# A gated cross-attention and expert layer on one core: the end of the attention reordered, the routing lists built in f16 pairs

## The chip, the core and the metric

The kernel runs on one core of one Trainium2 chip. The metric is the device time of one execution in microseconds (us). A core has TensorE (PE in the rows; PEld is its weight load), VectorE (DVE), ScalarE (ACT), GpSimd (POOL) and SyncE (SP), each with its own list of instructions, kept in step by semaphores; the DMA engines move data beside them.

## What is computed

Inputs: x (4 x 512 x 256, so 2048 tokens), a context of 4 x 1601 rows, for every token an index into its context, two gates, and weights. In short:

```python
# x = x + tanh(g_xattn) * attention(layernorm(x))
q = heads(layernorm(x) @ Wq.T)                       # 16 heads of 16
k, v = split(ctx @ Wkv.T)
rows = clip(index - [0, 1, 2, 3], 0)                 # 4 keys and values for a token
x = x + tanh(g0) * (softmax(q . k[rows] / 4) @ v[rows]) @ Wo.T
# x = x + tanh(g_ffn) * experts(layernorm(x))
p = softmax(layernorm(x) @ gate_w.T)                 # 8 experts, the best 2 of each token
for e in range(8):
    out += p_e * (silu(xn @ w1[e] + b1[e]) @ w2[e] + b2[e])
```

The indices of this input lie below 128, so only the first 128 context rows of each batch are projected.

## The kernel before, in words

**Tiles.** Tokens lie in T = 16 tiles of 128, on the partitions. Matrix products of the attention and of the router run in f32; those of the experts run in f16 with both factors split into a high and a low half.

**Start.** Keys and values of the first 128 context rows are projected for each batch b (PE line 813), copied from PSUM (ACT lines 632 and 692 for b = 0 and 2, VectorE line 1114 for 1 and 3) and stored to `near_rows_b` in DRAM (SP line 406). For every tile, GpSimd then issues a gather (line 515) of 128 windows of four rows, 1 MB, into one of 8 slots. Gathers 0 to 3 go out one behind the other, then the norms of tiles 4 to 15 (lines 467 to 473) are made, then gather u + 4 in step u. Gather 4 waits for all four stores (line 511). SP holds the first expert weights back until the four stores have landed (line 418).

**Attention loop, step t.** VectorE multiplies keys by queries (1128), reduces them to scores (1132), masks, takes the maximum and subtracts it; ScalarE takes Exp (651); VectorE normalizes (1153 to 1158); GpSimd multiplies the values by the probabilities (490; the second half of the last tile is VectorE's, 1165). TensorE turns and sums them in 16 matmuls (859, `aT`), ScalarE copies aT (670), TensorE projects (872), VectorE adds it to the residual `xs` (1146) and takes the statistics of the second norm (1149, 1169). GpSimd finishes that norm (495 to 503), ScalarE applies it (662: `x2`) and casts the high half (666), GpSimd makes the low half (525), ScalarE issues the store of the token to `tokens_split` (642). TensorE turns x2 (846), ScalarE copies it (686), TensorE makes the logits (838), ScalarE keeps them (681). Every engine runs this from one `step(t)`, with the lags of `second(t)`, `router(t)` and `norms_at(t)` (lines 296 to 323), up to t = T + 2; LATE = 12 is the tile from which the lags are shorter. Each step of SP, GpSimd, ScalarE and TensorE is thus an order fixed by the lags, and an engine stands at the first wait of that order that isn't met.

**Routing.** VectorE runs a chain of instructions that each wait for the one before (`link`): for the tiles below LATE, then for the last four, maximum, difference, Exp (ScalarE, 656 and 708), sum, the best two experts, one-hots (`choose`, 1188). TensorE counts members (901, 902), VectorE scans (1221) and derives how many tiles of 128 each expert fills, their order by size (1226 to 1237), and every token's slot, column (tile) and row (1240 to 1251). The list "which token is in which slot" is a matrix product of one-hots of 32 (tile, choice) pairs: rows (`row_tok`, 27 by VectorE in 1269, 5 by ScalarE in 723) times columns (1264) multiplied by the token number (GpSimd, 563). GpSimd also makes three small tables (555 to 558) and padding rows. TensorE sums the lists (910), VectorE makes `slot_row` (1285 to 1290). At the end a further chain finds for each tile the expert above its own (1293 to 1314 on VectorE, 937 and 939 on TensorE, `e_from` 747 on ScalarE, `e_prev` 566 on GpSimd).

**Experts.** Up to NT = 39 tiles; 37 are filled here. GpSimd gathers the tokens of a tile (587), TensorE turns them (991), VectorE copies them (1334, `xT`), TensorE multiplies up (963) and down (977 to 985), ScalarE applies silu (759), VectorE splits the result (1323, 1325) and weights it (1348, 1351), GpSimd adds it to the output in DRAM (595). The weights arrive in f32 (SP, 371: 16 transfers) and are split in 32 units: ScalarE the high half (739), VectorE the low half (1308), two units ahead of the first tile and then one a tile. The split starts only when all weights are there (`w_in`, 742).

```python
# line 510, GpSimd, gather of tile u
if u == 4:
    for b in range(1, B):
        pool.wait_ge(s[f"kv_out{b}"], 16)
# line 1269, VectorE, one-hots of the rows
count(v.tensor_tensor(row_tok[:, first:last, :], spread_mid(iota[:, :], n),
                      r_row[:, first:last].rearrange("p (n o) -> p n o", o=1).to_broadcast([P, n, P]),
                      ALU.is_equal))
```

## Time and profile before

| | us |
|---|---|
| median of 3 runs | 382.8 (382.32 to 383.78) |
| the profiled execution, its own time | 385.14 |
| its span, first to last instruction | 383.4 |
| TensorE busy | 313.2 (82%) |
| VectorE busy | 273.8 (71%) |
| GpSimd busy | 214.9 (56%) |
| ScalarE busy | 174.4 (45%) |

Busy shares are means over stages that differ much. The mean granted TensorE clock is 0.907 of full speed; 1.00 is 2.4 GHz, 0.5 is 1.2 GHz. In a row of the timeline the first number is the start in us from the span's start, the second the duration, then engine, line, operation, output<-input, and in brackets how long the engine was idle before it and what released it. A merged row (x16) gives the time from its first start to its last end.

### The profile page before, as it was taken

To read this page: it belongs to the slowest core of one execution; us is meant where nothing else is said; L and a number is where in the kernel's file an instruction comes from. 1 tells how busy PE (TensorE), PEld (TensorE's weight loads), DVE (VectorE), ACT (ScalarE), POOL (GpSimd) and SP (SyncE) were. 2 spreads that over 40 slices of the span, in tenths; PEclk is the share of its full clock that TensorE was granted. 3 is DMA by queue.
4 is the path that set the end of the run, shared out by engine and by line. 5 is a ranking of instruction groups with operands and counts; after the bars stand their busy time and mean duration, and the time that the engine had idled before them with its cause. 6 is when DMAs were issued, how large, how long until landed. Compare 5 with 4: busy or idle time off the path is not lost.

```text
span 383.4 us, 10814 instructions
## 1 busy us (share of the span) xinstructions
PE 313.2 (82%) x3163; PEld 255.6 (67%) x3163; DVE 273.8 (71%) x636; ACT 174.4 (45%) x490; POOL 214.9 (56%) x234
## 2 busy tenths in 40 slices
PE   3753999999885121999999999999999999999830
PEld 3432888888773120988888888888888888777610
DVE  3856699999914884597878778887787887565510
ACT  2430255555434253565556556555654644344200
POOL 1365588886763184526574766667477566633240
PEclk9985999999976555799999999999999999999985
DMA  7598999999599800203332342323233233222121
GB/s 224 194 358 331 383 358 335 412 350 363 169 345 376 263 1 22 54 14 59 43 57 45 45 66 38 58 39 59 49 53 46 47 57 56 40 52 29 19 29 14
DMA packets 31388, 53.20 MB, mean 139 GB/s; under 512 B 4818, under 2 KB 25538, under 8 KB 29284
## 3 DMA queue, kind: packets, MB, share of 16 engines
q0 software_dynamic: 9408, 26.63, 27.7%
q1 hardware_dynamic: 16100, 22.57, 17.0%
q10 hardware_dynamic: 5824, 3.26, 2.8%
q8 instruction: 33, 0.54, 0.6%
q14 instruction: 23, 0.19, 0.1%
HBM read 42.29 MB, written 10.17 MB: 137 GB/s over the span
## 4 chain that ended last, share of the span: by engine, by line
PE 70%; POOL 7%; issue 7%; DVE 5%; DMA 4%; ACT 3%; POOLq 0%; SPq 0%; ACTq 0%; DVEq 0%
PE ps L963 25%; PE ps L977 14%; PE ps L980 7%; PE ps L859 6%; PE ps L872 3%; DMA near_rows<-w_parts 2%; PE ps L991 2%; PE ps L813 2%; POOL sel L490 2%; PE ps L985 2%; PE ps L831 2%; DMA w_parts<-in_L_xattn_Wkv 1%; PE ps L838 1%; ACT aT L670 1%; PE ps L984 1%
## 5 line engine op out<-in xcount | busy, mean ns | idle before, releaser
L963 PE MATMUL ps<-sel,w_parts 128*128 128x128 f16 x1776 | 142.1, 221 | 0.6 <-DVE sel L1334 0.6
L963 PEld LDWEIGHTS ps<-sel,w_parts 128*128 x1776 | 120.7, 99 | 25.1 <-issue 0.9
L759 ACT ACTIVATE sel<-ps,b1T 128x128 f32<-128x128 f32 x296 | 84.5, 369 | 92.2 <-PE ps L963 86.2
L595 POOL DMA_INDIRECT out<-sel x37 | 62.9, 1700 | 87.7 <-DVE sel L1351 72.2
L977 PE MATMUL ps<-w_parts,sel 128*128 x259 | 96.3, 379 | 2.0 <-DVE sel L1325 1.7
L980 PE MATMUL ps<-w_parts,sel 128*128 x259 | 70.6, 273 | 0.0
L1325 DVE SCALAR_TENSOR_TENSOR sel<-sel 128x512 f16<-128x512 f32 x74 | 51.3, 693 | 2.5
L587 POOL DMA_INDIRECT sel<-tokens_split,sel x37 | 44.8, 1210 | 7.5 <-POOL sel L582 5.9
L1308 DVE SCALAR_TENSOR_TENSOR w_parts<-w_parts x32 | 39.0, 1220 | 9.2 <-issue 7.9
L582 POOL TENSOR_TENSOR sel<-sel 128x1 f32<-128x1 f32 x37 | 39.3, 1062 | 2.4 <-PE ps L991 2.4
L1323 DVE TENSOR_SCALAR sel<-sel 128x512 f16<-128x512 f32 x74 | 33.6, 455 | 9.3 <-ACT sel L759 9.2
L739 ACT ACTIVATE w_parts<-w_parts x32 | 33.9, 1067 | 10.2 <-issue 5.3
L1334 DVE COPY sel<-ps 128x512 f16<-128x512 f16 x37 | 15.7, 425 | 30.8 <-PE ps L991 21.2
L977 PEld LDWEIGHTS ps<-w_parts,sel 128*128 128x128 f16 x259 | 25.3, 98 | 7.5 <-issue 2.9
L980 PEld LDWEIGHTS ps<-w_parts,sel 128*128 128x128 f16 x259 | 25.3, 98 | 3.5
L872 PE MATMUL ps<-WT,aT 128*128 128x256 f32 x64 | 18.9, 420 | 4.7 <-ACT aT L670 4.5
L859 PE MATMUL ps<-ident,sel 128*128 128x128 f32 x128 | 17.5, 294 | 5.9 <-POOL sel L490 5.9
L859 PEld LDWEIGHTS ps<-ident,sel 128*128 128x128 f32 x128 | 16.6, 208 | 6.8 <-POOL sel L490 6.6
L831 PE MATMUL ps<-WT,xnT 128*128 128x256 f32 x64 | 17.6, 399 | 4.0 <-ACT xnT L676 4.0
L1348 DVE TENSOR_SCALAR xn<-ps,sel 128x256 f32<-128x256 f32 x37 | 17.7, 479 | 3.0 <-PE ps L985 2.9
L1146 DVE SCALAR_TENSOR_TENSOR xs<-ps,tanh_g,xs 128x256 f32<-128x256 f32 x16 | 7.6, 476 | 16.2 <-PE ps L872 16.2
L525 POOL TENSOR_TENSOR xsplit<-x,xsplit 128x256 f16<-128x256 f32 x16 | 11.2, 703 | 14.1 <-ACT xsplit L666 13.0
(215 smaller groups left out, 470.2 us busy)
## 6 DMA issues: line engine op xcount, KB each, us to landing
w_parts<-in_L_ffn_w SPq DMA_DIRECT2D x16, 1024.0 KB
out<-xs SPq DMA_DIRECT2D x16, 128.0 KB
tokens_split<-xsplit ACTq DMA_DIRECT2D x16, 128.0 KB, 5.9
xs<-in_x SPq DMA_DIRECT2D x3, 512.0 KB, 11.2
near_rows<-w_parts SPq DMA_DIRECT2D x4, 256.0 KB, 6.9
sel<-tokens_split,sel POOLq DMA_INDIRECT x37
out<-sel POOLq DMA_INDIRECT x37
w_parts<-in_ctx ACTq DMA_DIRECT2D x1, 512.0 KB, 4.0
```

The source lines that it names most:

```text
L582: pool.tensor_tensor(slot_w[:, at(q + 1)], xg[(k + 1) % 4][:, bass.ds(e + D, 1)], valid[:, at(q + 1)], ALU.mult).then_inc(s["slot_w_ok"], 1)
L587: pool.indirect_dma_start(xg[k], None, xd, bass.IndirectOffsetOnAxis(slot_row[:, at(q + 4)], 0))\
L595: pool.indirect_dma_start(out_rows, bass.IndirectOffsetOnAxis(slot_row[:, at(q - 1)], 0), y_sb[(k + 3) % 4], None, compute_op=ALU.add).the ...
L739: act.activation(part(to, 0), place(raw), ACT.Copy, scale=W_SCALE).then_inc(s["w_hi_ok"], 1)
L759: act.activation(h32[n][:, c * P:c * P + P], ps_h[n][:, c * P:c * P + P], ACT.Silu, bias=biases[:, c:c + 1], scale=1.0 / (X_SCALE * W_SCALE))\
L859: mm = pe.matmul(ps_a[:, c * P:c * P + P], slot(t - 1)[:, j, D + c * P:D + c * P + P], ident[:, :], start=(j == 0), stop=(j == WIN - 1))
L963: mm = pe.matmul(ps_h[n][:, c * P:c * P + P], w, xx, start=(i == 0), stop=(i == len(products) - 1))
L977: pe.matmul(sides, hi, both, start=(c == 0), stop=False)
L980: mm = pe.matmul(ps_y[n][:, 0:D], lo, rhi, start=False, stop=False)
L1308: v.scalar_tensor_tensor(out=part(to, 1), in0=place(raw), scalar=W_SCALE, in1=part(to, 0), op0=ALU.mult, op1=ALU.subtract).then_inc(s["w_l ...
L1323: v.tensor_scalar(h_hi[n][:, cols], h32[n][:, cols], H_SCALE, None, ALU.mult).then_inc(s["hhi_ok"], 1)
L1325: v.scalar_tensor_tensor(out=h_lo[n][:, cols], in0=h32[n][:, cols], scalar=H_SCALE, in1=h_hi[n][:, cols], op0=ALU.mult, op1=ALU.subtract). ...
```

## The change

- **Start.** ScalarE copies batches 0 and 1, VectorE 2 and 3. Gather 4 waits for its own store only (batch 1). Gather 0 goes out, then the norms of tiles 4 to 15, then gathers 1 to 3. SP no longer holds the first weights back; weights 11 to 15 go out in step 13, when the last gather has landed, 7 to 10 as their slots come free. Two small VectorE instructions (`gate2`, `b2_lo`) move behind step 0.
- **Drain.** `step(t)` runs to tile 14; what follows is written out as a list of calls on each engine. Turns and logits of the last four tiles use PSUM banks of their own.
- **Routing.** The scan runs on VectorE over the one-hots before the members are counted; sums and the rank matrix are accumulated in PSUM by TensorE (`ps_members`, `ps_row`, `ps_base`), two links of VectorE's chain go. The one-hots of rows and columns and the product with the token number are made by VectorE with f16 operands, laid out so that two neighbours lie next to each other (`spread_pairs`, `over_pairs`). The tables move to VectorE, the padding to ScalarE and TensorE; GpSimd has nothing left in the routing.
- **Behind the list.** The chain for the experts above runs behind the first tile's copy of xT (VectorE, q = -2), in tiles 0 and 2 (ScalarE, TensorE). The first four tiles read fixed places; one register load less on ScalarE and VectorE for the first expert.

The core of the diff (SP, GpSimd, ScalarE, TensorE, VectorE in this order; the ScalarE list of the steps before tile 14 has the old order):

```diff
-                sp.wait_ge(s[f"kv_ok{b % 2}"], b // 2 + 1)
+                sp.wait_ge(s[f"kv_ok{b // 2}"], b % 2 + 1)
...
+                if now and t % 2 == 0 and t < 14:
                     sp.wait_ge(s["kprod"], t + 1)
-                    if t == 0:
-                        for b in range(B):
-                            sp.wait_ge(s[f"kv_out{b}"], 16)
-                        sp.wait_ge(s["wT_ok"], 2)
-                    weights_in(sp, t // 2 if t < 14 else 11)
-                if t == T:
-                    sp.wait_ge(s["kprod"], T)
-                    for u in range(12, T):
-                        weights_in(sp, u)
+                    weights_in(sp, t // 2)
+                if t == 1:
+                    sp.wait_ge(s["b2_hi_ok"], 1)
+                    sp.wait_ge(s["b2_lo_ok"], 1)
+                    sp.dma_start(b2_split[0], b2_hi[:, :]).then_inc(s["b2_split_out"], 16)
+                    sp.dma_start(b2_split[1], b2_lo[:, :]).then_inc(s["b2_split_out"], 16)
...
+                if t == T + 1:
                     sp.wait_ge(s["aT_ps"], T)
-                    for u in range(7, 11):
-                        weights_in(sp, u)
+                    weights_in(sp, 10)
...
+                if t == 13:
+                    for b in range(B):
+                        sp.wait_ge(s[f"kv_out{b}"], 16)
+                    sp.wait_ge(s["wT_ok"], 2)
+                    sp.wait_ge(s["sel_in7"], 32)
+                    for u in range(11, T):
+                        weights_in(sp, u)
+                if 14 <= t <= T:
+                    sp.wait_ge(s["aT_ps"], t - 1)
+                    weights_in(sp, t - 7)
...
+            gather(0)
             first_norms(2, slice(TPB, T))
-            for t in range(T + 3):
-                step(t)
+            for u in range(1, 4):
+                gather(u)
+            for t in range(T - 1):
+                if t >= 1:
+                    values(t - 1)
+                if t >= 4 and t % 2 == 0:
+                    norms(t - 4, 2)
+                if t + 4 < T:
+                    gather(t + 4)
+                if t >= 4:
+                    remainder(t - 4)
+            values(T - 2)
+            norms(T - 4, 1)
+            remainder(T - 5)
+            values(T - 1)
+            norms(T - 3, 1)
+            remainder(T - 4)
+            norms(T - 2, 1)
+            remainder(T - 3)
+            norms(T - 1, 1)
+            remainder(T - 2)
+            remainder(T - 1)
...
-            table(pool.tensor_scalar(e_new[:, :], iota16[0:E, 0:NT], e_col[:, 0:1], None, ALU.is_equal))
-                some = col_hot[:, T * h:T * h + T, :]
-                pool.tensor_tensor(some, some, tok_f[:, :].rearrange("p (t o) -> p t o", o=1).to_broadcast([P, T, NT]),
-                                   ALU.mult).then_inc(s["col_ok"], 1)
-            pool.wait_ge(s["from_ok"], 1)
-            pool.tensor_scalar(e_prev[:, :], ones16[0:E, :], e_from[:, :], None, ALU.mult).then_inc(s["prev_ok"], 1)
...
+            pool.wait_ge(s["rt"], RT_TILES)
+            tiles = tile_count(pool)
             pool.wait_ge(s["rt"], RT_SLOT)
-
-            tiles = tile_count(pool)
...
+            token_out(T - 6)
+            logits_kept(T - 6)
+            second_x(T - 5)
+            first_half(T - 5)
+            exponentials(T - 1)
+            attended(T - 2)
+            second_turned(T - 5)
+            second_x(T - 4)
+            first_half(T - 4)
+            logits_kept(T - 5)
+            second_turned(T - 4)
+            token_out(T - 5)
+            logits_kept(T - 4)
+            second_x(T - 3)
+            attended(T - 1)
+            first_half(T - 3)
+            token_out(T - 4)
+            act.wait_ge(s["rt"], RT_SHIFT)
+            act.activation(r_ex[:, 0:LATE, :], r_tmp[:, 0:LATE, :], ACT.Exp).then_inc(s["rt_exp"], 1)
+            second_x(T - 2)
+            second_turned(T - 3)
+            token_out(T - 3)
+            logits_kept(T - 3)
+            second_turned(T - 2)
+            logits_kept(T - 2)
+            second_x(T - 1)
+            second_turned(T - 1)
+            logits_kept(T - 1)
+            for u in (T - 2, T - 1):
+                first_half(u)
             act.wait_ge(s["rt"], RT_SHIFT_LATE)
             act.activation(r_ex[:, LATE:T, :], r_tmp[:, LATE:T, :], ACT.Exp).then_inc(s["rt_exp"], 1)
 
+            for u in (T - 2, T - 1):
+                token_out(u)
...
+            act.wait_ge(s["row_ps"], 1)
+            act.activation(pad_row[:, :], ps_row, ACT.Copy).then_inc(s["row_ok"], 1)
+            act.wait_ge(s["row_ok"], 1)
+            for e in range(E):
+                act.activation(pad_hot[:, e, :], iota[:, :], ACT.Abs, bias=pad_row[:, e:e + 1], scale=-1.0)\
+                    .then_inc(s["pad_hot_ok"], 1)
             act.wait_ge(s["span_ps"], 1)
             act.activation(e_col[:, :], ps_span[0:E, 0:2], ACT.Copy).then_inc(s["span_ok"], 1)
-            act.wait_ge(s["pad_far_ok"], 3)
...
+                if q == 0:
+                    act.wait_ge(s["from_ps"], 1)
+                    act.activation(e_from[:, :], ps_from[0:E, 0:1], ACT.Copy).then_inc(s["from_ok"], 1)
+                    act.wait_ge(s["from_ok"], 1)
+                    act.activation(e_prev[:, :], ones16[0:E, :], ACT.Copy, scale=e_from[:, 0:1]).then_inc(s["prev_ok"], 1)
...
+            for t in range(1, T - 1):
+                query(t + 1)
+                values(t - 1)
+                if t + 2 < T:
+                    first_turn(t + 2)
+                if t >= 5:
+                    logits(t - 5)
+                outputs(t - 1)
+                if t >= 4:
+                    second_turn(t - 4)
+
+            logits(T - 6)
+            values(T - 2)
+            second_turn(T - 5)
+            outputs(T - 2)
+            second_turn(T - 4)
+            logits(T - 5)
+            values(T - 1)
+            logits(T - 4)
+            outputs(T - 1)
+            second_turn(T - 3)
+            logits(T - 3)
+            second_turn(T - 2)
+            logits(T - 2)
+            second_turn(T - 1)
+            logits(T - 1)
...
+            pe.wait_ge(s["rt"], RT_CUM)
+            last = r_cum[:, :, T - 1:T].rearrange("p e o -> p (e o)")
+            pe.matmul(ps_members, ones16[:, :], last, start=True, stop=True).then_inc(s["rt_ps"], 1)
+            pe.matmul(ps_row, ones16[:, :], last, start=True, stop=False)
+            pe.matmul(ps_row, far_ahead[:, :], r_m16[:, 0, :], start=False, stop=False)
+            pe.matmul(ps_row, ident16[:, :], row16[:, :], start=False, stop=True).then_inc(s["row_ps"], 1)
+            pe.matmul(ps_base, not_ahead[:, :], r_m16[:, :, :], start=True, stop=False)
+            pe.matmul(ps_base, ones16[:, :], r_cum[:, :, :].rearrange("p e t -> p t e"), start=False, stop=True)\
+                .then_inc(s["rt_ps"], 1)
...
+                    mm = pe.matmul(ps_list[:, 1:NT + 1], row_hot[:, n // 2, :, n % 2], col_tok[:, n // 2, :, n % 2],
+                                   start=(n == 0), stop=(n == 2 * T - 1))
...
+            rows_into_list(24, 2 * T).then_inc(s["list_ps"], 1)
...
+                if q == 2:
+                    pe.wait_ge(s["prev_ok"], 1)
+                    pe.matmul(ps_prev[:, 0:NT], e_prev[:, :], e_own[:, :], start=True, stop=True)\
+                        .then_inc(s["prev_ps"], 1)
...
+            shifted_logits(slice(0, LATE))
+            assert done[0] == RT_SHIFT
+            residual(T - 1)
+            second_moments(T - 1)
             choose(slice(0, LATE), 0)
+            shifted_logits(slice(LATE, T))
+            assert done[0] == RT_SHIFT_LATE
             choose(slice(LATE, T), 1)
-            assert done[0] == RT_PAIRS
-
+
+            link(v.tensor_tensor_scan(r_cum[:, :, :].rearrange("p e t -> p (e t)"), r_go[:, :, :].rearrange("p e t -> p (e t)"),
+                                      r_members, 0.0, ALU.mult, ALU.add))
+            assert done[0] == RT_CUM
...
-            link(v.tensor_tensor(r_base[:, :, :], ps_rank[:, 0:P].rearrange("p (t e) -> p t e", e=E),
-                                 r_exc[:, :, :].rearrange("p e t -> p t e"), ALU.add))
...
+            def spread_pairs(ap, n):
+
+                return ap.rearrange("p (n o i) -> p n o i", o=1, i=2).to_broadcast([P, ap.shape[1] // 2, n, 2])
+
+            def over_pairs(n, width):
+
+                return twice[:, 0:width, :].rearrange("p (o r) i -> p o r i", o=1).to_broadcast([P, n, width, 2])
+
+            halves_of = [slice(T // 2 * h, T // 2 * h + T // 2) for h in range(2)]
             for h in range(2):
-                some = slice(T * h, T * h + T)
-                count(v.tensor_tensor(col_hot[:, some, :], spread_mid(iota[:, 0:NT], T),
-                                      r_col[:, some].rearrange("p (n o) -> p n o", o=1).to_broadcast([P, T, NT]),
-                                      ALU.is_equal))
-            for first, last in ((0, 8), (8, 16), (16, 24), (24, ACT_ROWS)):
-                n = last - first
-                count(v.tensor_tensor(row_tok[:, first:last, :], spread_mid(iota[:, :], n),
-                                      r_row[:, first:last].rearrange("p (n o) -> p n o", o=1).to_broadcast([P, n, P]),
-                                      ALU.is_equal))
+                count(v.tensor_tensor(col_tok[:, halves_of[h], :, :], over_pairs(T // 2, NT),
+                                      spread_pairs(r_col[:, T * h:T * h + T], NT), ALU.is_equal))
+            for h in range(2):
+                dve.wait_ge(s["rt"], RT_HOT + 1 + h)
+                count(v.tensor_tensor(col_tok[:, halves_of[h], :, :], col_tok[:, halves_of[h], :, :],
+                                      spread_pairs(tok16[:, :], NT), ALU.mult))
+            for first in range(0, 2 * T, 8):
+                count(v.tensor_tensor(row_hot[:, first // 2:first // 2 + 4, :, :], over_pairs(4, P),
+                                      spread_pairs(r_row[:, first:first + 8], P), ALU.is_equal))
                 if first == 0:
                     assert done[0] == RT_ROWS
+                if first == 8:
+                    dve.wait_ge(s["span_ok"], 1)
+                    v.tensor_scalar(e_ended[:, :], iota[0:E, 0:NT], e_col[:, 1:2], None, ALU.is_ge).then_inc(s["tables"], 1)
+                    v.tensor_scalar(e_new[:, :], iota[0:E, 0:NT], e_col[:, 0:1], None, ALU.is_equal).then_inc(s["tables"], 1)
+                    dve.wait_ge(s["tables"], 1)
+                    v.scalar_tensor_tensor(out=e_own[:, :], in0=iota[0:E, 0:NT], scalar=e_col[:, 0:1], in1=e_ended[:, :],
...
-            dve.wait_ge(s["prev_ps"], 1)
-            link(v.tensor_copy(tile_p[:, :], ps_prev[:, 0:NT]))
-            assert done[0] == RT_LIST
...
+                if q == -2:
+                    experts_above()
+                if q == 2:
+                    dve.wait_ge(s["prev_ps"], 1)
+                    link(v.tensor_copy(tile_p[:, 4:NT], ps_prev[:, 4:NT]))
+                    assert done[0] == RT_PLACES
```

## Rows read from the trace of the kernel before

**Rows 1.** Waits, 14 to 152 us: waiter, released by: us in total, times, longest

```profile
DVE xs L1146 <- PE ps L872: 16.2, 3, 8.5
```

**Rows 2.** Stretches: us; busy us (instructions) of PE, PEld, DVE, ACT, POOL; clock; DMA; GB/s

```profile
62.00:81.00 19.00, 17.98 (x124) 16.01 (x124) 17.84 (x44) 10.66 (x32) 16.81 (x20) 1.00 1.01 386
111.70:118.10 6.40, 5.93 (x24) 5.13 (x23) 0.04 (x1) 1.22 (x4) 1.85 (x5) 0.52 1.07 386
...
200.00:250.00 50.00, 50.00 (x617) 40.68 (x616) 40.66 (x73) 29.00 (x81) 31.11 (x28) 1.00 0.32 51
```

**Rows 3.** Timeline of the start

```profile
22.55 0.69 DVE L1114 COPY w_parts<-ps 128x512 f32<-128x512 f32 x1 [3.74 <-PE ps L813]
...
23.67 0.41 DVE L1118 SCALAR_TENSOR_TENSOR b_lo<-x,b_hi 8x256 f16<-8x256 f32 x1
...
24.17 1.22 DVE L1128 TENSOR_TENSOR sel<-sel,ps 128x1024 f32<-128x1024 f32 x1
...
28.27 0.22 DVE L1158 TENSOR_TENSOR prob<-ps,rden 128x64 f32<-128x64 f32 x1
...
33.09 1.08 POOL L515 DMA_INDIRECT w_parts<-near_rows,win_near  x1 [6.99 <-DMA near_rows<-w_parts]
...
34.20 1.95 POOL L490 TENSOR_TENSOR sel<-sel,prob 128x1024 f32<-128x1024 f32 x1
...
41.35 0.48 DVE L1146 SCALAR_TENSOR_TENSOR xs<-ps,tanh_g,xs 128x256 f32<-128x256 f32 x1 [5.45 <-PE ps L872]
```

**Rows 4.** Line 406, the second store of near_rows, issued at 18.8 us

```profile
L406 SPq DMA_DIRECT2D near_rows<-w_parts x1: 332/332/332, 18.8 to 18.8; - x1
...
DMA to landing us min/median/max: 6.1/6.1/6.1
```

**Rows 5.** Timeline of the drain

```profile
104.77 2.03 PE L859 MATMUL ps<-ident,w_parts 128*128 128x128 f32 x16
...
107.19 1.05 POOL L490 TENSOR_TENSOR w_parts<-w_parts,prob 128x512 f32<-128x512 f32 x1
...
107.27 1.13 PE L872 MATMUL ps<-WT,aT 128*128 128x256 f32 x4 [0.47 <-ACT aT L670]
...
111.82 3.76 PE L859 MATMUL ps<-ident,w_parts 128*128 128x128 f32 x16
...
118.06 0.48 DVE L1146 SCALAR_TENSOR_TENSOR xs<-ps,tanh_g,xs 128x256 f32<-128x256 f32 x1 [8.46 <-PE ps L872]
...
119.04 0.18 DVE L1169 BATCH_NORM_AGGREGATE mv<-st 128x2 f32<-128x6 f32 x1
...
121.32 0.25 DVE L1196 TENSOR_REDUCE r_sum<-xn 128x12 f32<-128x96 f32 x1 [1.67 <-ACT xn L656]
...
125.53 0.18 ACT L681 ACTIVATE logit<-ps 128x8 f32<-128x8 f32 x1 [1.11 <-PE ps L838]
```

**Rows 6.** Timeline of the routing

```profile
134.53 2.45 ACT L717 ACTIVATE sel<-iota,pad_to 128x128 f16<-128x128 f32 x8 [1.19 <-POOL pad_to L553]
134.66 0.80 DVE L1264 TENSOR_TENSOR sel<-iota,r_col 128x624 f16<-128x624 f32 x1
...
136.10 4.05 DVE L1269 TENSOR_TENSOR sel<-iota,r_row 128x1024 f16<-128x1024 f32 x4
...
137.54 2.31 POOL L558 TENSOR_SCALAR e_new<-iota,e_col 8x39 f16<-8x39 f16 x1
...
149.00 1.14 POOL L587 DMA_INDIRECT sel<-tokens_split,sel  x1 [0.83 <-issue]
```

**Rows 7.** Timeline of the first expert tile

```profile
149.12 2.36 DVE L1308 SCALAR_TENSOR_TENSOR w_parts<-w_parts  x2 [2.02 <-issue]
...
152.97 0.42 DVE L1334 COPY sel<-ps 128x512 f16<-128x512 f16 x1 [1.38 <-PE ps L991]
...
153.54 0.71 PE L963 MATMUL ps<-sel,w_parts 128*128 128x128 f16 x5 [0.60 <-DVE sel L1334]
```

**Rows 8.** The page's list of DMA issues: KB each

```profile
w_parts<-in_L_ffn_w SPq DMA_DIRECT2D x16, 1024.0 KB
```

581 lines of the change are left out of this document (269 added, 312 removed).

## The prediction

> **What bounds the kernel now.** I read the waits of the stretch between the first loads and the first expert tile, to see who stands still: VectorE waits three times, 16.2 us in all, for one thing, the output projection of a token tile [rows 1]. Then the table by stretches [rows 2], where the reader is to see three regimes. In the attention loop VectorE works 17.84 of 19 us and the DMA engines are full (share 1.01, 386 GB/s). In the drain behind the last attention tile, VectorE works 0.04 of 6.4 us and TensorE's granted clock is 0.52, its level of 1.2 GHz. In the experts TensorE works 50.00 of 50 us at 2.4 GHz, and nothing of the change makes its matmuls fewer or shorter. So what the change can bring is how much earlier the first expert matmul starts, 153.54 us; behind it lie 229.9 us that I leave as they are. Next I read the timelines of the start [rows 3, 4], the drain [rows 5], the routing [rows 6] and the hand-over [rows 7]. All times below are of the profiled execution (385.14 us, span 383.4); the median of the runs is 2.3 us lower, and I take the same saving off it.
>
> **A, the start.** VectorE stands idle for 5.45 us ahead of the first residual at 41.35 [rows 3]. The chain behind it: GpSimd reaches the gather of tile 4 with probabilities ready since 28.49, but stands there 6.99 us until 33.09, because it also waits for the fourth near_rows store; only then it multiplies the values of tile 0 (34.20), and the residual comes 7.15 us after that. The change lets this gather wait for its own two stores alone; the second was issued at 18.8 and landed 6.1 us later, 24.9 [rows 4], before GpSimd is free. The chain then starts at 28.55 and ends at 35.7, and VectorE arrives at 35.9: the idle time goes whole, -5.45. Against it, two small instructions (the second of them 0.41 us, some 0.65 with gaps) move from before the first key product to behind step 0. The first product may start between the end of the copy, 23.24, and today's 24.17, depending on when gather 0 lands, which now has no company in its queue (gathers 1 to 3 move behind 3 us of norms). Net -0.2 to +0.65, I take +0.2. What is late next: gathers 1 to 3 are issued 3 us later and are wanted 4.3 us apart; if one is late, VectorE pays it. **A = -5.2**, between -6 and 0.
>
> **B, the loop.** VectorE's work of one step, not its waits, sets the pace [rows 2]. The new order puts the turn of the next input and the logits into the pause in which TensorE waits for the copy of aT. TensorE follows VectorE by less, which matters only in the drain. **B = -0.3**, between -0.6 and +1.
>
> **C, the drain** (in times of the trace of before). GpSimd is done with the last values at 108.24, yet TensorE takes them at 111.82, behind turns and logits of tiles 11 and 12, at the low clock: 3.76 us where the same sixteen took 2.03 at 104.77; the residual follows at 118.06 [rows 5]. In the new list the last Exp stands behind the logits and norms of tiles 10 and 11 on ScalarE, so the probabilities come about 1.3 us later; but GpSimd no longer does two remainders ahead of the values, which end near 107.7. TensorE has one turn and one set of logits between, starts at 108.5, needs 2.0, ScalarE puts the logits and x2 of two tiles ahead of the aT copy (1.7 with it), and the projection takes 1.13 as at 107.27: 113.4 instead of 118.0. VectorE's first `choose` sum waited on until 121.32, because its Exp stood on ScalarE behind x2 of tile 14; now the Exp is done by then and the sum follows the last moments, 114.7. It is hidden there by the late logits: from the last moments (119.2) to the last logits kept (125.71) passed 6.5 us. The written order leaves the GpSimd norm, one x2, one turn, one copy, the logits, 4.9 to 6.5 us; I take 5.2, so 119.9 against 125.71. The two f16 halves now ahead of the late Exp cost +0.35. **C = -5.4**, between -2 and -7.
>
> **D, routing.** From the last logits kept to the first one-hot passed 8.95 us (134.66). Two links of VectorE's chain go (r_exc, r_base, 0.3 us each with gaps) and the wait for the rank matmul lies under r_comb: about -0.9, so 8.05. One-hots: before, 3456 elements took 4.05 us at 136.10, 1.17 ns each [rows 6]. Now VectorE makes two column compares, two column products (2496 elements) and all 32 rows (4096): 7.7 us at that rate. With every operand 16 bits wide and read in pairs it may be half: the nearest rows are copies from PSUM of 512 elements, 0.69 us in f32 at 22.55 [rows 3] and 0.42 in f16 [rows 7], 0.52 ns less for each element. I take half, 4.0. The trace has no two-input f16 instruction on VectorE, so both ends stay: 3.3 and 7.7.
> By the Trainium skill ("VectorE: DVE Perf Modes", the perf-mode tier table) a tensor_tensor with 16-bit operands runs at twice the rate of f32. The Trainium skill also speaks against this form: "Vector Engine (DVE) Microarchitecture Reference", section 5.2, has a stream without two adjacent 4-byte words at up to 1.73 ns a column instead of 1.05; a pair read again and again is one such word, and by that rule the one-hots would cost 2.2 us more. No row here shows a pair; the rows at 136.10 re-read a single 4-byte word at 1.17 ns.
> Then: three table instructions 0.6, two memsets 0.1, five links for order and tile count 1.15, four links for the slots 0.95, GpSimd's issue 0.4. In all 4.0 + 3.2 = 7.2 us from first one-hot to first gather, where it was 14.3 (134.66 to 149.00). Half of those 14.3 hung on GpSimd: its e_new alone took 2.31 us at 137.54, the column products came after it, and e_prev kept it until shortly before 149.00. All of that leaves it. Cost nothing: TensorE's last eight list matmuls (under the five links), and ScalarE's eight Abs (2.45 at 134.53), Relu and copies, which start when the row sums stand in PSUM, near 124.6, and are wanted at 134.2; without that cover they would cost some 4. **D = -8.0**, between -4.3 and -9.5.
>
> **E, hand-over.** Before, gather to first matmul was 4.54 us with the splits of VectorE (149.12, 2.4 us for two) under the gather's flight [rows 7]. Now the slots are out 0.4 us before VectorE is free, and it stands 1 to 2 us for its register loads (2.02 at 149.12; one load less now), splits 2.4, loads the tile count and copies xT. It ends 0.6 us behind the gather. **E = +0.6**, between 0 and +2. The links for the experts above (1.2 us) go behind that copy, where VectorE next waits for ScalarE's split and the second turn for about as long; the two small matmuls and waits in tiles 0 and 2 cost 0.1.
>
> **Sum**: -5.2 - 0.3 - 5.4 - 8.0 + 0.6 = -18.3. The profiled execution would come to 385.1 - 18.3 = 366.8, the median to 382.8 - 18.3 = **364.5 us**.
>
> **Rivals.** (1) *The pairs gain nothing*: 7.7 us instead of 4.0, 368.2. For: no row shows the form; against: the halved copy. The skill's rule of adjacent words is a milder form of it, 366.7. (2) *The DMA engines take the start back.* They are full in the loop [rows 2]; the first weights, held until now by the four stores, go out behind the first key product, amid gathers 1 to 3. If VectorE waits for gathers 1, 2 or 3, or each of twelve steps stretches by 0.4 us (a step moves 1.8 MB, so some 8% less than the 386 GB/s), A is gone: 369.7. Against: a gather goes out four steps, 19 us, ahead of its use. (3) *The drain's list is wrong in one place*: the last Exp behind x2 of tile 11 drags values, residual and norms, or the clock falls as before and late logits keep their 6.5 us: C is -2, 368. (4) *Slower: the weights come last.* Nine 1 MB transfers [rows 8] are issued from tile 13's step on; with the outputs and tokens 11.4 MB from 88 us. ScalarE can't split unit 0 before all have landed, and it now wants them near 128 instead of 145. At 386 GB/s they are there at 118; each microsecond beyond 128 costs one, and only from 149 on, under 190 GB/s, is the kernel slower. 386.
>
> **How the numbers follow.** Forecast 0.62 (own range 361 to 367.5), pairs 0.12, DMA 0.13, drain 0.10, late weights 0.03. The four sooner cases all gain over 12 us, far beyond the 0.5% (1.9 us) that a measurement here tells from no change. Range 361 to 370: it takes in rivals 1 to 3 alone, not two of them at once. Faster 0.95, same 0.02, slower 0.03.
>
> **What would show it.** Right: no idle VectorE ahead of the first residual and the fourth key product near 37.6; last residual input near 108 (113.4 - 5.5); last logits kept near 114.5; a 1024-element one-hot at 0.6 us; first gather at 130, first expert matmul near 135, experts 230 us. Wrong: VectorE waiting for gathers early, one-hots at 1.1 us, ScalarE idle ahead of its first split with DMAs flying, or TensorE gaps between expert tiles.

## The result, and the profile after

The changed kernel takes 364.7 us, median of 4 runs (363.52 to 365.81), against 383.16 (382.32 to 383.78) of the kernel before in runs beside it: ratio 0.9519, 95% interval 0.9483 to 0.9555. Forecast: 364.5 (361 to 370), faster. Its profiled execution took 364.77 us, span 363.1, at its own median; that of before, 385.14 us, lay 2.0 us above the 383.16 given here (2.3 above the 382.8 of the forecast). So the traces differ by 20.3 us of span, the medians by 18.5.

The first expert matmul starts at 132.52 us instead of 153.54, 21.0 sooner. Behind it 230.6 us pass to the end, 229.9 before. I read the same views in the same order. Stretches of the kernel after (columns as in [rows 2]):

```profile
103.84:107.30 3.46, 2.41 (x18) 2.04 (x16) 0.01 (x2) 1.93 (x6) 2.57 (x7) 1.00 1.07 360
106.00:112.00 6.00, 3.71 (x19) 2.59 (x20) 4.46 (x43) 3.02 (x10) 1.92 (x6) 0.88 1.09 379
124.00:130.00 6.00, 1.76 (x32) 1.17 (x28) 4.53 (x18) 2.27 (x3) 1.33 (x2) 0.50 0.01 1
180.00:230.00 50.00, 50.00 (x616) 40.62 (x614) 40.70 (x72) 29.48 (x81) 31.50 (x27) 1.00 0.31 50
```

In the drain VectorE's wait for the last residual is the stretch from 103.84 to 107.30: 3.46 us with TensorE's clock at 1.00. In the wait of the kernel before it was 0.52 [rows 2]. Behind the residual (106 to 112, for the most part) VectorE has `choose` to do and works 4.46 of 6 us. The DMA engines are idle by 124 (1 GB/s). The experts are unchanged.

**Start**, timeline of the kernel after, answering to [rows 3]:

```profile
24.07 1.22 DVE L1207 TENSOR_TENSOR sel<-sel,ps 128x1024 f32<-128x1024 f32 x1 [0.91 <-DMA sel<-near_rows,win_near]
...
26.59 0.94 POOL L514 DMA_INDIRECT w_parts<-near_rows,win_near  x1 [0.30 <-issue]
...
28.48 2.09 POOL L489 TENSOR_TENSOR sel<-sel,prob 128x1024 f32<-128x1024 f32 x1 [0.95 <-DVE prob L1232]
...
29.01 1.22 DVE L1207 TENSOR_TENSOR sel<-sel,ps 128x1024 f32<-128x1024 f32 x1 [0.24 <-DMA sel<-near_rows,win_near]
...
33.58 1.22 DVE L1207 TENSOR_TENSOR sel<-sel,ps 128x1024 f32<-128x1024 f32 x1 [0.25 <-DMA sel<-near_rows,win_near]
...
36.77 0.47 DVE L1241 SCALAR_TENSOR_TENSOR xs<-ps,tanh_g,xs 128x256 f32<-128x256 f32 x1
...
38.38 1.19 DVE L1207 TENSOR_TENSOR sel<-sel,ps 128x1024 f32<-128x1024 f32 x1
```

The fourth key product of the kernel before:

```profile
42.97 1.19 DVE L1128 TENSOR_TENSOR sel<-sel,ps 128x1024 f32<-128x1024 f32 x1
```

Gather 4 goes out at 26.59 instead of 33.09, values of tile 0 start at 28.48 instead of 34.20, the residual finds VectorE busy: no idle time in its row, where 5.45 us stood. New are three waits of VectorE for gathers 0, 1 and 2, 1.40 us in all. The fourth key product starts at 38.38 instead of 42.97. The 0.91 us for gather 0 are no net cost: they lie where two small instructions stood, and the first key product starts at 24.07 as it did at 24.17. What is lost is 0.49 us, for gathers 1 and 2.

**Drain**. The last key product starts at 95.57 (first row), before it was 100.59 (second). Then the timeline of the kernel after, answering to [rows 5]:

```profile
95.57 1.19 DVE L1207 TENSOR_TENSOR w_parts<-w_parts,ps 128x1024 f32<-128x1024 f32 x1
```

```profile
100.59 1.19 DVE L1128 TENSOR_TENSOR w_parts<-w_parts,ps 128x1024 f32<-128x1024 f32 x1
```

```profile
100.82 1.56 POOL L489 TENSOR_TENSOR w_parts<-w_parts,prob 128x512 f32<-128x512 f32 x1 [0.17 <-DVE prob L1232]
...
102.63 2.03 PE L893 MATMUL ps<-ident,w_parts 128*128 128x128 f32 x16
...
106.06 1.13 PE L902 MATMUL ps<-WT,aT 128*128 128x256 f32 x4 [1.05 <-ACT aT L652]
...
107.30 0.48 DVE L1241 SCALAR_TENSOR_TENSOR xs<-ps,tanh_g,xs 128x256 f32<-128x256 f32 x1 [3.46 <-PE ps L902]
...
108.38 0.22 DVE L1291 TENSOR_REDUCE r_sum<-xn 128x12 f32<-128x96 f32 x1
...
112.88 0.18 ACT L684 ACTIVATE logit<-ps 128x8 f32<-128x8 f32 x1 [1.11 <-PE ps L926]
```

The sixteen matmuls of the last tile take 2.03 us where they took 3.76, the residual waits 3.46 us instead of 8.46, `choose` (r_sum) goes on at once, and the last logits are kept at 113.06 (112.88 + 0.18), 12.65 us sooner.

**Routing and hand-over**, timeline of the kernel after, answering to [rows 6, 7]:

```profile
121.38 0.47 DVE L1368 TENSOR_TENSOR sel<-twice,r_col 128x624 f16<-128x624 f16 x1
...
122.95 1.29 DVE L1375 TENSOR_TENSOR sel<-twice,r_row 128x1024 f16<-128x1024 f16 x2
...
127.34 2.00 ACT L780 ACTIVATE w_parts<-w_parts 128x1024 f16 x2 [2.01 <-DVE sel L1399]
...
128.37 1.10 POOL L576 DMA_INDIRECT sel<-tokens_split,sel  x1 [12.74 <-DVE sel L1408]
...
129.36 2.36 DVE L1426 SCALAR_TENSOR_TENSOR w_parts<-w_parts 128x1024 f16<-128x1024 f16 x2 [1.16 <-ACT w_parts L780]
...
131.31 0.61 PE L1062 MATMUL ps<-ident,sel 128*128 128x128 f16 x4 [4.91 <-DMA sel<-tokens_split,sel]
...
131.96 0.42 DVE L1449 COPY sel<-ps 128x512 f16<-128x512 f16 x1 [0.24 <-PE ps L1062]
```

First one-hot to first gather: 7.0 us (121.38 to 128.37), where it was 14.3. Two row instructions of 1024 elements take 1.29 us together.

### The profile page after: what moved, and what is told of

It is laid out like the page before. It is cut to its first block, busy times and chain, and to the rows that moved or that the text cites. A ratio compares the mean times of both kernels' runs of the same rounds, so it can differ in the third digit from the quotient of the medians.

```text
span 363.1 us, 10808 instructions
## 1 busy us (share of the span) xinstructions
PE 308.9 (85%) x3168; PEld 252.7 (70%) x3168; DVE 270.9 (75%) x641; ACT 172.6 (48%) x486; POOL 204.8 (56%) x226
## 4 chain that ended last, share of the span: by engine, by line
PE 66%; POOL 10%; DVE 8%; issue 6%; DMA 6%; ACT 2%; POOLq 0%; SPq 0%; ACTq 0%; DVEq 0%
PE ps L1034 27%; PE ps L1048 15%; PE ps L1051 8%; PE ps L893 3%; DMA sel<-near_rows,win_near 3%; PE ps L1062 2%; PE ps L1056 2%; POOL w_parts L489 2%; POOL sel L489 2%; PE ps L902 2%; DMA w_parts<-in_L_xattn_Wkv 2%; POOL sel L514 1%; PE ps L1055 1%; PE ps L1050 1%; POOL rstd L499 1%
## 5 line engine op out<-in xcount | busy, mean ns | idle before, releaser
L576 POOL DMA_INDIRECT sel<-tokens_split,sel x37 | 42.0, 1136 | 19.4 <-DVE sel L1408 12.7
L1426 DVE SCALAR_TENSOR_TENSOR w_parts<-w_parts (+1 forms) x32 | 39.0, 1220 | 8.6 <-issue 6.4
L571 POOL TENSOR_TENSOR sel<-sel 128x1 f32<-128x1 f32 x37 | 40.3, 1090 | 3.4 <-PE ps L1062 3.4
L780 ACT ACTIVATE w_parts<-w_parts (+1 forms) x32 | 34.1, 1067 | 7.9 <-issue 4.3
L489 POOL TENSOR_TENSOR sel<-sel,prob 128x1024 f32<-128x1024 f32 x8 | 15.6, 1952 | 6.3 <-DVE prob L1232 6.3
L1062 PE MATMUL ps<-ident,sel 128*128 128x128 f16 x148 | 14.8, 224 | 4.9 <-DMA sel<-tokens_split,sel 4.9
```

The source lines that it names most:

```text
L571: pool.tensor_tensor(slot_w[:, at(q + 1)], xg[(k + 1) % 4][:, bass.ds(e + D, 1)], valid[:, at(q + 1)], ALU.mult).then_inc(s["slot_w_ok"], 1)
L576: pool.indirect_dma_start(xg[k], None, xd, bass.IndirectOffsetOnAxis(slot_row[:, at(q + 4)], 0))\
L780: act.activation(part(to, 0), place(raw), ACT.Copy, scale=W_SCALE).then_inc(s["w_hi_ok"], 1)
L1426: v.scalar_tensor_tensor(out=part(to, 1), in0=place(raw), scalar=W_SCALE, in1=part(to, 0), op0=ALU.mult, op1=ALU.subtract).then_inc(s["w_l ...
```

## The experiments

Every ratio is to the kernel before on the same chip; its interval reaches 0.003 to 0.005 to each side, 1.2 to 1.9 us. The changed kernel itself stands at 0.9519, and at 0.9509 in a repeat on the chip on which all but the first four kernels ran; a difference given as a range is against the one and the other. Plain medians against the repeat put `d_old`, `h_single`, `h_pool` and `w_old` 6.2, 3.7, 1.9 and 4.7 us above it, 1 to 2 us more than their ratios do; a size below is no surer than that.

### The start: the wait, the order of the gathers, the early weights

The trace gives the whole gain at the start to gather 4's wait. The change also moved gathers 1 to 3 behind the norms and released the first weights, so each is put back alone, then together.

`s_wait`, gather 4 waits for all four stores again:

```diff
+                if u == 4:
+                    for b in range(1, B):
+                        pool.wait_ge(s[f"kv_out{b}"], 16)
```

> The changed kernel with one thing put back: GpSimd waits for all four stores of near_rows before gather 4. Theory 1 (the wait itself was the cost): the values of tile 0 start 3 to 5 us later than their 28.48, VectorE stands idle again ahead of the first residual, the time is 3 to 5 us over the changed kernel's 364.7. Rival (the fourth store was late only because gathers 1 to 3 were queued ahead of it, and the new order of the gathers cures that by itself): the store lands by 28.5 and the time stays within 1 us of 364.7.

Measured: 366.1 us, ratio 0.9533 (0.9501 to 0.9566).

`s_gathers`, gathers 0 to 3 ahead of the norms again, the new wait kept:

```diff
-            gather(0)
+            for u in range(4):
+                gather(u)
             first_norms(2, slice(TPB, T))
-            for u in range(1, 4):
-                gather(u)
```

> The changed kernel with gathers 0 to 3 one behind the other again, ahead of the norms of tiles 4 to 15. Theory 1 (the order costs nothing either way, the DMA engines are full and deliver the same bytes): VectorE's waits for gathers 0 to 2 (0.91, 0.24, 0.25 us in the changed kernel) shrink to under 0.5 us in sum, the time is within 1 us of 364.7. Rival (the order is what lets the fourth store and gather 4 through): gather 4 or the values of tile 0 come later and the time is 2 to 5 us longer.

Measured: 364.72 us, ratio 0.9497 (0.9466 to 0.9528).

`s_both`, both of these edits:

> Both put back: the wait for all four stores and gathers 0 to 3 ahead of the norms. Theory 1 expects what the wait alone gives, or up to 1 us more, 368 to 370, with the gather of tile 4 at 33 as in the kernel before. Rival expects most of the loss only here: 369 to 371, where each alone gave under 1 us.

Measured: 371.36 us, ratio 0.9682 (0.9643 to 0.9722).

`s_old`, both, and, as before, weights held until the four stores have landed (the edit shown) and the two small VectorE instructions ahead of step 0:

```diff
                     sp.wait_ge(s["kprod"], t + 1)
+                    if t == 0:
+                        for b in range(B):
+                            sp.wait_ge(s[f"kv_out{b}"], 16)
                     weights_in(sp, t // 2)
```

> The start as before in all four points: the two above, the first weights held back until the four stores have landed, the two small instructions ahead of step 0. Measures the whole of the start. By the sum on record 5.2 us are given back (369.9); by the traces of before and after 4.6 us (369.3). The theory that the early weights crowd the gathers expects this one to be 0.5 to 1 us better than the run with the two alone; if they don't, they are equal within 0.5 us.

Measured: 371.62 us, ratio 0.9671 (0.9638 to 0.9705).

Alone, the wait costs 0.5 to 0.9 us and the order -0.8 to -0.5, which is inside the intervals; together they cost 6.3 to 6.6. `s_old` is no slower than `s_both`. That doesn't show that held weights and the place of the small instructions are worth nothing: VectorE's third key product starts at 32.51 in `s_old` and 33.56 in `s_both`, and the wait for the residual takes the difference up (6.99 us against 5.74). The place of the two instructions is tried without that wait in `best1`; held weights were not tried without it. Why the two act only together is in the line of the stores. The fourth store of near_rows in `s_wait` (first fence) and in `s_both` (second), duration, start, and below it the time from issue to landing:

```profile
L397 SPq DMA_DIRECT2D near_rows<-w_parts x1: 320/320/320, 23.2 to 23.2; - x1
...
DMA to landing us min/median/max: 4.1/4.1/4.1
```

```profile
L397 SPq DMA_DIRECT2D near_rows<-w_parts x1: 320/320/320, 23.1 to 23.1; - x1
...
DMA to landing us min/median/max: 10.1/10.1/10.1
```

A store of 256 KB lands after 4.1 us when gather 0 (1 MB) is ahead of it and gather 1 has just been issued (22.93), after 10.1 us when four have. The early weights aren't the cause: in `s_old`, which holds them back, it is 9.2. Timelines of `s_wait`, then of `s_both`:

```profile
28.17 0.94 POOL L517 DMA_INDIRECT w_parts<-near_rows,win_near  x1 [1.66 <-DMA near_rows<-w_parts]
```

```profile
34.04 1.08 POOL L517 DMA_INDIRECT w_parts<-near_rows,win_near  x1 [7.58 <-DMA near_rows<-w_parts]
...
42.57 0.48 DVE L1243 SCALAR_TENSOR_TENSOR xs<-ps,tanh_g,xs 128x256 f32<-128x256 f32 x1 [5.74 <-PE ps L904]
```

With the late gathers GpSimd waits 1.66 us for all four stores and is still in time for the probabilities; with the early ones it waits 7.58, and VectorE pays 5.74. One thing flatters `s_wait`: VectorE waited 2.95 us for gather 0 there, so the probabilities were late themselves. With those of the changed kernel (28.39) the values, free to start near 29.2, would be up to 0.8 us late, an estimate from these rows. The Trainium skill ("DMA: Bandwidth & Descriptors", section on queues, rings and completion order) has the increment of a DMA's semaphore land only after every earlier write of the same DMA engine, across its queues. The direction agrees with 10.1 against 4.1 us; no run here separates that from sharing the engines' time.

### The drain

`d_old`, every engine's list of the drain as before, with the lags of `second(t)`, `router(t)`, `norms_at(t)` and the shared PSUM banks; start and routing stay new:

```diff
-            for t in range(1, T - 1):
-                query(t + 1)
...
+            for t in range(1, T + 3):
+                if t + 1 < T:
+                    query(t + 1)
+                order = router(t)
...
+                for kind, u in order:
+                    (logits if kind == "logits" else second_turn)(u)
```

> The changed kernel with the drain of before: the steps run on to the last lag on GpSimd, ScalarE, TensorE and VectorE, the late turns and logits in the banks of the others. Start and routing stay new. By the two traces the drain gave 7.6 us (last logits kept 12.65 earlier, less the 5.0 of start and loop): 372.3. By the sum on record, 5.4 us: 370.1. Rival (part of the drain's gain hangs on the start or would come anyway, since TensorE's clock and the DMA load differ now): 2 to 4 us, 367 to 369.

Measured: 371.01 us, ratio 0.9641 (0.9595 to 0.9686), 4.7 us above the changed kernel by ratio against its first 0.9519, 5.1 against its repeat. The order within the loop is the old one too; the weights go out as in the changed kernel. Timeline of `d_old`:

```profile
96.05 1.19 DVE L1166 TENSOR_TENSOR w_parts<-w_parts,ps 128x1024 f32<-128x1024 f32 x1
...
106.41 0.61 PE L897 MATMUL ps<-gateT,x2T 128*128 128x8 f32 x4 [0.47 <-ACT x2T L688]
...
106.88 2.03 PE L873 MATMUL ps<-ident,w_parts 128*128 128x128 f32 x16
...
109.38 1.13 PE L882 MATMUL ps<-WT,aT 128*128 128x256 f32 x4 [0.47 <-ACT aT L661]
...
110.55 0.48 DVE L1200 SCALAR_TENSOR_TENSOR xs<-ps,tanh_g,xs 128x256 f32<-128x256 f32 x1 [5.48 <-PE ps L882]
...
118.02 0.18 ACT L693 ACTIVATE logit<-ps 128x8 f32<-128x8 f32 x1 [1.11 <-PE ps L897]
```

The last logits come at 118.02 instead of 112.88, so the written lists are worth 5.1 us in this trace: 0.5 in the loop (the last key product at 96.05 against 95.57) and 4.7 behind it. The kernel before, with the same old list, took 3.0 us longer than `d_old` from the last key product to the last logits (24.9 against 22.0). Its rows:

```profile
110.95 1.02 PE L838 MATMUL ps<-gateT,x2T 128*128 128x8 f32 x4 [0.47 <-ACT x2T L686]
...
116.05 1.97 PE L872 MATMUL ps<-WT,aT 128*128 128x256 f32 x4 [0.47 <-ACT aT L670]
```

Three groups of matmuls make up the 3.0: the logits (1.02 us against 0.61), the sixteen (3.76 against 2.03) and the projection (1.97 against 1.13). The granted clock was 0.50 from 111.8 to 115.6 in the kernel before, and 1.00 from 106.8 to 109 in `d_old`. So of the 7.6 us that the drain gained from trace to trace, 4.7 are its list and 3.0 the clock. Over the executions of before the clock and the time go together: those with a mean granted clock of 0.907 or less took 385.1 to 386.7 us, those with 0.915 or more 381.5 to 384.6.

### The one-hots

`h_single`: the same instructions, f16 throughout, but each value once and its index re-read over a row, without the pairs:

```diff
-                return twice[:, 0:width, :].rearrange("p (o r) i -> p o r i", o=1).to_broadcast([P, n, width, 2])
+                return spread_mid(iota16[:, 0:width], n)
```

> The one-hots and column products in f16 as in the changed kernel and all on VectorE, but laid out singly as before, so that the innermost step of one input is 0. Theory (the pairs are what halves the time): a 1024-element compare takes 1.05 to 1.15 us instead of 0.65, a 624-element one 0.72 instead of 0.39, together 3 to 3.5 us more, 368. Rival (16-bit operands alone do it): no difference. If TensorE's reading of every second element in the paired layout cost something, its list matmuls, 0.45 us for eight, get shorter here.

Measured: 368.49 us, ratio 0.9576 (0.9525 to 0.9627), 2.2 to 2.6 us above the changed kernel.

`h_pool`: the products of the columns with the token number on GpSimd again, in the paired layout:

```diff
-            for h in range(2):
-                dve.wait_ge(s["rt"], RT_HOT + 1 + h)
-                count(v.tensor_tensor(col_tok[:, halves_of[h], :, :], col_tok[:, halves_of[h], :, :],
-                                      spread_pairs(tok16[:, :], NT), ALU.mult))
```

> The column products go back to GpSimd, in the new paired layout, all else as in the changed kernel. Theory 1 (the two engines slow each other, and the list waits for GpSimd): a product takes over 1.2 us on GpSimd beside VectorE's compares, those get longer than 0.65 us, the list starts 0.5 to 2 us later and the time is 0.5 to 2 us longer, even though VectorE has 0.8 us less to do. Rival (GpSimd hides it): 0.5 to 0.8 us shorter.

Measured: 366.64 us, ratio 0.9518 (0.9469 to 0.9566). By ratio the same, by median 1.9 us above the repeat: unclear. Its trace has 8.6 us from first one-hot to first gather (122.28 to 130.86) instead of 7.0.

The groups of instructions in the stretch of the one-hots (busy us, mean ns of one), of the changed kernel, of `h_single` and of `h_pool`:

```profile
L1375 DVE TENSOR_TENSOR sel<-twice,r_row 128x1024 f16<-128x1024 f16 x4 | 2.6, 679 | 0.0
L1372 DVE TENSOR_TENSOR sel<-sel,tok 128x624 f16<-128x624 f16 x2 | 0.9, 476 | 0.0
```

```profile
L1374 DVE TENSOR_TENSOR sel<-iota,r_row 128x1024 f16<-128x1024 f16 x4 | 4.7, 1212 | 0.0
```

```profile
L1378 DVE TENSOR_TENSOR sel<-twice,r_row 128x1024 f16<-128x1024 f16 x4 | 4.6, 1193 | 0.0
L559 POOL TENSOR_TENSOR sel<-sel,tok 128x624 f16<-128x624 f16 x2 | 3.0, 1534 | 6.7 <-DVE sel L1375 6.7
```

f16 without pairs gains nothing over f32 operands (1212 ns here, 1.24 us for each of three in the kernel before); pairs bring 679. And GpSimd's product beside them costs more than it takes off: of the four row compares the two that met it lasted up to 1715 ns, those clear of it 672. The Trainium skill ("SBUF — State Buffer", section "Who interferes with whom") has a VectorE instruction with two inputs from SBUF contend with a GpSimd instruction that reads SBUF, for ports that only one of the two holds at a time; the trace agrees in kind: 3.0 us of products on GpSimd took 2.1 us from the two compares beside them (3.35 us for two, 1.28 for the two clear of it).

### The weights

`w_old`, the last nine weight transfers nearly as before (11 in step 13, where it was 14; 12 to 15 behind the loop, 7 to 10 when the last values are turned):

```diff
-                    weights_in(sp, 10)
+                    for u in range(7, 11):
+                        weights_in(sp, u)
...
-                    for u in range(11, T):
-                        weights_in(sp, u)
-                if 14 <= t <= T:
-                    sp.wait_ge(s["aT_ps"], t - 1)
-                    weights_in(sp, t - 7)
+                    weights_in(sp, 11)
+                if t == T:
+                    for u in range(12, T):
+                        weights_in(sp, u)
```

> The last nine weight transfers issued as before, weight 11 in step 13, 12 to 15 and 7 to 10 behind the last tile of the loop. Tests rival 4, that the weights come last. In the changed kernel the DMA engines fall silent near 121 us and ScalarE wants the weights at 127.3. Issued from 96 us on they need 23 us at 387 GB/s and land near 122 to 128. Expectation: within 1 us of 364.7 if they land before 127, and a microsecond for each microsecond beyond; the first split of ScalarE shows it.

Measured: 369.44 us, ratio 0.9588 (0.9538 to 0.9637), 2.6 to 3.0 us above the changed kernel. Stretches, then the timeline, of `w_old`:

```profile
124.00:130.00 6.00, 2.65 (x41) 1.77 (x38) 5.42 (x20) 0.54 (x2) 0.00 (x0) 0.50 1.08 357
```

```profile
131.69 2.00 ACT L780 ACTIVATE w_parts<-w_parts 128x1024 f16 x2 [4.83 <-DMA w_parts<-in_L_ffn_w]
...
132.98 2.36 DVE L1426 SCALAR_TENSOR_TENSOR w_parts<-w_parts 128x1024 f16<-128x1024 f16 x2 [3.26 <-ACT w_parts L780]
133.07 2.11 POOL L576 DMA_INDIRECT sel<-tokens_split,sel  x1 [15.90 <-issue]
...
137.02 0.61 PE L1062 MATMUL ps<-ident,sel 128*128 128x128 f16 x4 [9.09 <-DMA sel<-tokens_split,sel]
137.67 0.42 DVE L1449 COPY sel<-ps 128x512 f16<-128x512 f16 x1 [2.32 <-PE ps L1062]
```

From 124 to 130 the DMA engines move 357 GB/s where the changed kernel has 1. ScalarE's first split waits 4.83 us for the weights. But that wait doesn't set the first expert matmul: VectorE has its splits done at 135.34 and then stands 2.32 us for the turn of the gathered tokens. The first gather is what comes last. The slots (VectorE's last cast, 129.55 + 0.17) were written by 129.7; the gather also waits for the 64 KB store of the routing weights into `tokens_split` (line 757). Issued at 119.25, it needed 12.3 us beside the weights (6.6 in the changed kernel) and landed near 131.6; the gather goes out 1.5 us behind it.

So the late weights cost 2.6 to 3.0 us by ratio once start and drain are faster. What their new places would give in the kernel before was not run.

### What could still be gained

Two things in the trace after: the 1.40 us of waits for gathers, and 1.05 us in which TensorE waits for the last aT copy, behind logits 12 and x2 of tile 13 on ScalarE. Four kernels on one chip, six runs each.

`after_again`, the changed kernel:

> The changed kernel itself, unaltered, as the yardstick for the three variants beside it. Every theory: ratio 0.952 of the kernel before, first expert matmul near 132.5 us, three waits of VectorE for gathers of 0.9, 0.24 and 0.25 us in the first steps, one of TensorE of 1.05 us for the last aT copy.

Measured: 364.77 us (364.58 to 366.06), ratio 0.9509 (0.9474 to 0.9545).

`swap_drain`:

```diff
+            exponentials(T - 1)
             second_x(T - 5)
             first_half(T - 5)
-            exponentials(T - 1)
...
+            attended(T - 1)
             logits_kept(T - 4)
             second_x(T - 3)
-            attended(T - 1)
```

> The changed kernel with two swaps in ScalarE's list of the drain: the last Exp ahead of x2 and half of tile 11, and the last aT copy ahead of logits 12 and x2 of tile 13. Theory (the chain values, aT, projection, residual still sets the drain, and ScalarE's place of the two costs 0.9 and 1.0 us of it): last residual 0.9 to 1.5 us sooner than 107.3, first expert matmul near 131.5, 0.9 us off the time, ratio 0.0024 below the changed kernel. Rival (the delayed x2 of tiles 11 and 13 push the late logits back by as much, so the last logits stay at 113.1): same time within 0.3 us although the last residual comes sooner.

Measured: 364.68 us (363.13 to 366.3), ratio 0.9504 (0.9467 to 0.9541).

`best1`, these swaps and `gate2`, `b2_lo` back ahead of step 0:

```diff
+            v.tensor_scalar(gate2[:, :], tanh_g[:, 1:2], W_UNSCALE * W_SCALE, None, ALU.mult)
...
             for t in range(T):
                 step(t)
-                if t == 0:
...
-                    v.tensor_scalar(gate2[:, :], tanh_g[:, 1:2], W_UNSCALE * W_SCALE, None, ALU.mult)
```

> The two swaps of the drain and, at the start, the two small instructions (gate2, b2_lo) back ahead of the first key product, where VectorE waits 0.9 us for gather 0 anyway. Theory (the 0.65 us of those two instructions fits into that wait): fourth key product 0.6 us sooner than 38.4, in all 1.5 us off the changed kernel, ratio 0.004 below it. Rival (gathers 1 and 2, not VectorE's work, set the next two products, which then wait by as much longer): start unchanged, waits for gathers 1 and 2 grow from 0.5 to 1.1 us in sum, and the time is that of the kernel with the drain's swaps alone.

Measured: 364.28 us (363.52 to 365.24), ratio 0.9492 (0.9457 to 0.9526).

`swap_both`, as `best1`, and gather 1 right behind gather 0:

```diff
             gather(0)
+            gather(1)
             first_norms(2, slice(TPB, T))
-            for u in range(1, 4):
+            for u in range(2, 4):
                 gather(u)
```

> As the kernel with the swaps and the early small instructions, and with gather 1 issued right behind gather 0, ahead of GpSimd's norms; gathers 2 and 3 stay behind them. Theory (gather 1 was late only because it was issued 3 us after gather 0): wait for gather 1 gone, the first product up to 0.5 us later as the two share the queue, fourth key product near 37.6, 0.3 to 0.6 us below the kernel without the move. Rival (the DMA engines are full there, so a gather issued sooner delays another by as much; the stores of near_rows 1 to 3 come later and gather 4 with them): nothing gained, or GpSimd waits up to 1 us at gather 4 and the residual of tile 0 with it.

Measured: 363.4 us (362.71 to 363.99), ratio 0.9459 (0.9425 to 0.9492). Timeline of `swap_drain`, then of `swap_both`:

```profile
105.00 1.13 PE L902 MATMUL ps<-WT,aT 128*128 128x256 f32 x4
...
106.23 0.48 DVE L1241 SCALAR_TENSOR_TENSOR xs<-ps,tanh_g,xs 128x256 f32<-128x256 f32 x1 [2.53 <-PE ps L902]
```

```profile
23.87 0.69 DVE L1199 COPY w_parts<-ps 128x512 f32<-128x512 f32 x1 [1.02 <-PE ps L858]
...
29.56 1.21 DVE L1208 TENSOR_TENSOR sel<-sel,ps 128x1024 f32<-128x1024 f32 x1
```

The swaps do in the trace what was expected: TensorE's wait is gone, residual (106.23 against 107.66) and last logits (111.83 against 113.25) come 1.4 us sooner than in the repeat, 0.9 of it behind the last key product, which itself came 0.5 sooner. The median doesn't show it (-0.1), and the six runs spread over 3.2 us: not settled. In `best1` the waits for gathers stay (0.25, 0.90 and 0.46, in sum 1.61; 1.68 in the repeat), so the small instructions' place gains nothing: the gathers' landing sets these products, as the rival had it. `swap_both` has no such wait at all, even at its second key product (29.56, after a copy that in this execution came 1.1 us late). But `d_old`, with gather 1 late as in the changed kernel, has no such wait either, after a copy at 24.19; so the late copy may be the reason. All six of its runs lie below all six of the repeat, the medians 1.4 us apart, the ratios by 0.005; their intervals overlap at the edge. It has the lowest median of the study; that the place of gather 1 is the cause is not shown.

## Why the prediction was right, and where it was not

The saving on the profiled execution was put at 18.3 us and came to 20.3 in the span; the medians moved by 18.5. That the forecast met the median within 0.2 us is in part luck: the execution that I subtracted from was 2.0 us above the median of its kernel, and 3.0 us of its drain were TensorE's low clock, which `d_old` didn't have.

| | forecast | trace |
|---|---|---|
| A, start | -5.2 (-6 to 0) | -4.6 |
| B, loop | -0.3 (-0.6 to +1) | -0.4 |
| C, drain | -5.4 (-7 to -2) | -7.6 |
| D, routing | -8.0 (-9.5 to -4.3) | -8.0 |
| E, hand-over | +0.6 (0 to +2) | -0.4 |
| from the first expert matmul on | 0 | +0.7 |

**A** (key product 42.97 to 38.38) held. Of the 0.6 us short of it, 0.49 are what I had priced at nothing: gathers 1 to 3 issued late, "if one is late, VectorE pays it". A part of rival 2 thus came true, at 0.5 us and not 5.2; whether the early weights have a share in it is open. What I gave as the cause was half of it. Priced alone, the wait for four stores was to be worth the 5.45 us; `s_wait` shows that it is worth next to nothing once the gathers stand behind the norms, and `s_gathers` the reverse. Either edit of the pair removes the stall.

**B**: last key product 100.59 to 95.57, 5.0 sooner, of which 4.6 are A's. The other 0.4 are the new order: from the fourth key product to the last pass 57.6 us before and in `d_old` (38.42 to 96.05), 57.2 in the changed kernel and in its repeat.

**C** was mis-sized beyond its own bound: -12.65 at the last logits, less 5.0 of A and B. Against my 5.8 up to there (125.71 to 119.9) that is 1.8 more. The step that failed: "TensorE has one turn and one set of logits between, starts at 108.5". In times of the trace of before it started at 107.6 (102.63 + 5.0), right behind GpSimd's values, since turn and logits were already done: 0.9 us. The way over the aT copy took 1.4 us and not 1.7, and the late logits behind the last moments (108.46) 4.6 us, below my 4.9 to 6.5: 0.3 and 0.6. Before, they took 6.5. That isn't the clock: the last turn and logits took 0.69 and 1.02 us now, 0.66 and 1.02 then. The tile's norm now starts on GpSimd 0.1 us behind the moments, where a remainder held it for 1.4, and its turn starts 0.65 us after x2 does, where it waited 1.26, behind a cast and logits on ScalarE.

What I did not see is how much of my own sum was clock. "Needs 2.0" for sixteen matmuls that had taken 3.76, and 1.13 for a projection that had taken 1.97, put 2.6 us on a full clock, without a reason why it should be full. `d_old` has the full clock with the old list, so these 2.6 (3.0, measured) can't be put down to the list. The list itself I had at 3.2 us up to the last logits, and it gave 4.7. Why the clock was low in the one execution of the old list and full in the other stays open. In all twelve traces with the new list the sixteen matmuls took 2.03 us; whether the new list helps the clock, two traces of the old one can't say.

**D** agreed in sum and roughly in its parts. Last logits kept to first one-hot: 8.3 us for 8.05. One-hot to gather: 7.0 for 7.2. The pairs cost 679 ns for 1024 elements, where I took half of 1.17 ns an element, 600. By `h_single`, where 3.4 us more passed between one-hot and gather, the pairs are worth 3.4 us in the trace and 2.2 to 2.6 in the ratios: rival 1, including the milder form after the Trainium skill ("Vector Engine (DVE) Microarchitecture Reference", section 5.2), is refuted (that section's table gives 1.73 ns for one source that hops at every element and up to 2.51 for other patterns; none of its rows reads one word again and again). A 4-byte word read again and again, when it holds two f16 values, isn't slowed here: 0.66 ns an element with all fixed cost. What is left of the 7.3 us lies in GpSimd's work leaving the chain; of it only the column products were tried, 1.6 us in the trace. The tables (e_new) were not put back, and their share is argued.

**E** had the wrong sign. I let VectorE stand 2 us for register loads ahead of its splits; it waited 1.16 us for ScalarE's split and finished it at 131.72, before TensorE's turn at 131.31 + 0.61 had ended. The gather to first matmul took 4.15 us against 4.54.

**Rival 3** (one wrong place in the drain's list): small and real, 1.05 us at the aT copy, inside a gain larger than forecast. **Rival 4** (weights last) did not occur: By the bytes moved behind 118 us (145 GB/s over 9.1 us, 1.3 MB at 390 GB/s) the weights were there near 121.5; ScalarE starts at 127.34, 6 us of slack. `w_old` makes the weights late: ScalarE's other condition was met there at 128.7 (VectorE's line 1399, 128.51 + 0.20), the weights at 131.7, 2.8 us later. Yet it does not show the price of a microsecond for each, since a longer wait lay beside it. The first expert matmul came 5.7 us later than in the changed kernel (138.23): 1.5 stood already at the last logits (114.42 against 112.88), 3.2 are the gather, held by the store of the routing weights, and 1.0 the way from gather to matmul (5.16 us against 4.15). What the weights delay first is a small store behind them, which I had not counted.

## What to carry to other kernels

Before a stall is priced by the wait that the trace names, ask why what it waits for is late: here the same stall (5.7 us of VectorE) could be removed by not waiting for a store or by not queueing 4 MB of gathers ahead of it, and taking both bought no more. Before a drain is priced from one trace, see at which clock its matmuls ran, and whether the change gives a reason for another. Where several engines drain together, write their last steps as one list by the time each input comes, and move the transfers that the next stage wants along with it; otherwise part of the gain is lost to them and to the small stores beside them. Compares and products of one-hots in f16 ran fast here only with their neighbours in pairs, and with no elementwise GpSimd work beside them.
